# A graph attention pair on one core: scores of the second layer from h times (Wq'Wk) times h, keys made a chunk ahead

## The chip, the cores and the metric

One core of one Trainium2 chip runs the whole program. The metric is the device time of one execution in microseconds; the median of three runs is given. Engines: TensorE (PE), VectorE (DVE), ScalarE (ACT), GpSimd (POOL) and SyncE (SP), which issues most of the DMAs.

## The reference

Two layers over 8192 nodes with 128 features and one dense 0/1 matrix adj (8192 x 8192, int32):

```python
h = relu(layernorm(x))                       # layer 0: graph attention
wh = h @ W; e = leaky(wh @ a1 + (wh @ a2).T, 0.2); e = where(adj > 0, e, -9e15)
x = x + elu(softmax(e) @ wh)
h = relu(layernorm(x))                       # layer 1: cosine attention
Qn, Kn = cos_normalize(h @ Wq.T), cos_normalize(h @ Wk.T)   # x / max(norm, 1e-4)
att = softmax(where(adj > 0, Kn @ Qn.T, -9e15))
x = x + 0.5 * (mask * (att @ h) + (1 - mask) * h) + 0.5 * h # mask: the row has a neighbour
```

## The kernel before

The matrix adj is read twice, once for each layer, 1 MB at a time into slots of a ring.

**Layer 0** goes over eight chunks of 1024 rows; a chunk has 32 units of 2 x 128 neighbours. For each unit SP loads adj into one of 8 slots (L265), ScalarE turns it into 0/1 (Sign, L406), VectorE makes the weights with two operations (L808), and TensorE runs 48 matmuls (L1020) on f16 words split in a high and a low part. Each engine runs its own instruction queue in program order and waits on semaphores. VectorE and ScalarE do the epilogue of chunk c in pieces between the masks of chunk c+1 (quotient, elu, residual, LayerNorm, h split in two f16 parts in u_buf), at the units given in `parts`; x1 and h are written to DRAM.

**The transition.** Layer 1 needs, for all 8192 nodes, the normalised q and k, transposed, in q_buf and k_buf, each as two f16 parts. The nodes go in 16 blocks of 512. For a block SP loads h from DRAM (load_h, L286), TensorE transposes it (t2, L951, in f32), ScalarE copies the result (copy_ht, L496), TensorE multiplies with Wq' and Wk' side by side in f32 (qk, L1047), ScalarE squares the product (square, L510), VectorE sums the squares (norms, L822), ScalarE takes roots (root, L520), VectorE forms reciprocals and scales the product (scaled, L833), TensorE transposes q and k (t3, L1058), ScalarE copies the high parts (high, L515 and L516) and VectorE subtracts for the low parts (low, L840). GpSimd takes no part in this. The epilogue of the last chunk of layer 0 lies between blocks 0 to 7. One buffer holds the squares. The first two transpositions of h (t2) stand before the last group of eight units of layer 0. Layer 1 begins when block 15 is done.

**Layer 1** goes over 16 chunks of 512 rows, each with 16 steps of 4 x 128 neighbours: TensorE makes scores of a step in four banks (L1086, 12 matmuls of 512 columns in two halves), ScalarE exponentiates each half with one instruction over 1024 columns (exps, L554), VectorE masks with adj (L866), ScalarE rounds to f16 (high_part, L560), VectorE subtracts (low_part, L871), and TensorE multiplies with the h parts in u_buf (values, L1102 and L1107). The values run LAG = 3 steps behind the scores, so in the very first chunk scores of four steps come before the first values. Scores of a half wait for the exponentials of the same half one step earlier (s_e). The epilogue of a chunk is laid between the steps of the next (`parts` in chunk1).

Semaphores that matter below: s_used (unit consumed, frees a slot), s_ht and s_htc (h transposed, copied), s_sq (squares ready), s_lo (low parts ready), s_s, s_e, s_m, s_ph, s_pl (stages of a layer 1 step), s_hw (h written).

## Time and profile before

| | us |
|---|---|
| median of 3 runs (lowest to highest) | 2204.03 (2203.57 to 2205.78) |
| the profiled execution | 2204.63 |
| its span, first to last instruction | 2202.8 |
| TensorE matmuls busy | 2155.7 (98%) |
| VectorE busy | 1983.9 (90%) |
| ScalarE busy | 1641.0 (74%) |
| mean granted TensorE clock | 0.995 of 2.4 GHz |
| moved by DMA | 573.23 MB |

The sum of the busy times is no bound by itself: layer 0, the transition and layer 1 have different limits, and each stretch has to be looked at alone. Times in the rows are microseconds from the start of the span unless they are means in ns; L followed by a number is a line of the kernel.

### The profile page before, as it was taken

What the parts mean: (1) busy time and instruction counts of PE and PEld (TensorE: products, weight loads), DVE (VectorE), ACT (ScalarE), POOL (GpSimd) and SP (SyncE); (2) the same over time, 40 slices, a digit from 0 to 9 for tenths busy, and PEclk for the clock granted to TensorE, in tenths of its full rate; (3) what the DMA queues carried; (4) which work ended last, traced back from release to release, by engine and by line L of the source; (5) the groups of instructions that cost most, each with busy time, mean ns of one, the idle gap of its engine ahead of it and who ended that gap; (6) DMA issues with size and microseconds to landing.
All of it is one profiled execution on the core that took longest, in us unless ns stands there. A gap on an engine that the chain in (4) does not pass through costs nothing.

```text
span 2202.8 us, 62846 instructions
## 1 busy us (share of the span) xinstructions
PE 2155.7 (98%) x26133; PEld 1749.5 (79%) x26133; DVE 1983.9 (90%) x1701; ACT 1641.0 (74%) x1446; POOL 9.5 (0%) x25
## 2 busy tenths in 40 slices
PE   5999999999999979999999999999999999999998
PEld 5999999999999966777777777777777777777776
DVE  7999999999999799888888898898898888888887
ACT  6687778878787667777777777777777777777776
POOL 1000000000000000000000000000000000000000
PEclk9999999999999999999999999999999999999999
DMA  6899999999999824565665665656666656655653
GB/s 244 331 380 400 397 401 400 399 404 400 401 400 391 343 72 157 199 211 205 206 219 196 211 219 192 222 207 201 215 199 217 206 201 215 211 205 206 221 195 115
DMA packets 153483, 573.23 MB, mean 260 GB/s; under 512 B 9889, under 2 KB 10337, under 8 KB 152929
## 3 DMA queue, kind: packets, MB, share of 16 engines
q1 hardware_dynamic: 144096, 549.78, 68.6%
q10 hardware_dynamic: 9216, 20.98, 2.4%
q8 instruction: 132, 2.16, 0.4%
q14 instruction: 39, 0.31, 0.0%
HBM read 558.11 MB, written 12.62 MB: 259 GB/s over the span
## 4 chain that ended last, share of the span: by engine, by line
PE 94%; DVE 3%; ACT 1%; issue 1%; DMA 0%; SPq 0%; DVEq 0%; POOL 0%; ACTq 0%; POOLq 0%
PE bank L1020 32%; PE bank L1086 30%; PE bank L1107 21%; PE bank L1102 10%; DVE hl_buf L833 1%; PE bank L1047 0%; DVE hl_buf L645 0%; DVE hl_buf L657 0%; DVE norm L822 0%; DVE v_buf L840 0%; DVE q_buf L840 0%; DMA wqk_sb<-wqk 0%; ACT ring L554 0%; PE bank L951 0%; PE bank L1058 0%
## 5 line engine op out<-in xcount | busy, mean ns | idle before, releaser
L554 ACT ACTIVATE ring<-bank 128x1024 f32<-128x1024 f32 x512 | 523.7, 1023 | 348.8 <-PE bank L1086 346.5
L866 DVE SCALAR_TENSOR_TENSOR ring<-ring 128x2048 f32<-128x2048 int32 x256 | 586.4, 2291 | 158.7 <-ACT ring L554 158.7
L1020 PE MATMUL bank<-v_buf,ring 128*128 128x129 f16 (+1 forms) x12288 | 710.9, 220 | 6.3 <-DVE ring L808 6.1
L1020 PEld LDWEIGHTS bank<-v_buf,ring 128*128 128x128 f16 x12288 | 707.4, 98 | 9.8 <-issue 9.0
L1086 PE MATMUL bank<-v_buf,q_buf 128*128 128x512 f16 x3072 | 704.8, 379 | 2.3 <-ACT ring L554 1.3
L1107 PE MATMUL bank<-u_buf,hl_buf 128*128 (+1 forms) x8192 | 704.3, 220 | 0.0
L1107 PEld LDWEIGHTS bank<-u_buf,hl_buf 128*128 128x128 f16 x8192 | 631.9, 98 | 55.8
L808 DVE SCALAR_TENSOR_TENSOR ring<-r_ring,th_word,ring 128x1024 f32<-128x1024 f32 x512 | 619.8, 1276 | 22.7 <-ACT ring L406 22.3
L871 DVE TENSOR_TENSOR hl_buf<-ring,hl_buf 128x2048 f16<-128x2048 f32 x256 | 584.5, 2284 | 0.0
L1102 PE MATMUL bank<-u_buf,hl_buf 128*128 (+1 forms) x2048 | 557.9, 272 | 0.2 <-DVE hl_buf L871 0.2
L406 ACT ACTIVATE ring<-ring 128x2048 f32<-128x2048 int32 x256 | 481.2, 1908 | 94.5 <-DMA ring<-adj 90.9
L1086 PEld LDWEIGHTS bank<-v_buf,q_buf 128*128 (+1 forms) x3072 | 289.8, 98 | 305.4 <-issue 2.5
L560 ACT ACTIVATE hl_buf<-ring 128x2048 f16<-128x2048 f32 x256 | 487.0, 1902 | 0.6 <-DVE ring L866 0.6
L1102 PEld LDWEIGHTS bank<-u_buf,hl_buf 128*128 128x128 f16 x2048 | 197.0, 96 | 30.3 <-DVE hl_buf L871 0.4
L1047 PE MATMUL bank<-wqk_sb,hl_buf 128*128 128x256 f32 x128 | 34.2, 414 | 10.0 <-DVE hl_buf L833 9.6
L1047 PEld LDWEIGHTS bank<-wqk_sb,hl_buf 128*128 128x128 f32 x128 | 24.6, 202 | 16.3 <-ACT hl_buf L496 7.6
L465 ACT ACTIVATE hl_buf<-q_buf,nbias,rstd 128x128 f32<-128x128 f32 x64 | 25.9, 483 | 10.8 <-DVE nbias L636 10.8
L421 ACT ACTIVATE v_buf<-hl_buf 128x516 f16<-128x516 f32 x16 | 10.1, 639 | 25.0 <-DVE hl_buf L733 25.0
L951 PE MATMUL bank<-ident,hl_buf 128*128 128x128 f32 x128 | 21.5, 299 | 6.5 <-POOL hl_buf L357 4.1
L439 ACT ACTIVATE hl_buf<-bank,den 128x128 f32<-128x128 f32 x64 | 17.3, 381 | 10.5 <-DVE den L750 10.5
L951 PEld LDWEIGHTS bank<-ident,hl_buf 128*128 128x128 f32 x128 | 16.8, 154 | 9.5 <-POOL ident L348 4.1
L1058 PE MATMUL bank<-ident,hl_buf 128*128 128x128 f32 x128 | 18.5, 291 | 5.7 <-DVE v_buf L840 5.7
(106 smaller groups left out, 451.2 us busy)
## 6 DMA issues: line engine op xcount, KB each, us to landing
ring<-adj SPq DMA_DIRECT2D x512, 1024.0 KB, 5.7
r_ring<-a_rows SPq DMA_DIRECT2D x8, 512.0 KB, 7.1
x_dram<-q_buf ACTq DMA_DIRECT2D x8, 512.0 KB, 7.0
h_dram<-hl_buf ACTq DMA_DIRECT2D x8, 512.0 KB, 7.2
hl_buf<-h_dram SPq DMA_DIRECT2D x16, 256.0 KB, 2.7
r_ring<-x_dram ACTq DMA_DIRECT2D x16, 256.0 KB, 3.9
r_ring<-h_dram ACTq DMA_DIRECT2D x16, 256.0 KB, 4.1
out<-r_ring ACTq DMA_DIRECT2D x16, 256.0 KB, 4.4
```

The lines of the kernel that those rows point to most:

```text
L406: nc.scalar.activation(slot(k), slot(k, I32), ACT.Sign).then_inc(s_sg, 1)
L554: nc.scalar.activation(p_ring[:, k, hf * 1024:(hf + 1) * 1024], bank[:, 2 * hf:2 * hf + 2, :].rearrange("p b n -> p (b n)"), ACT.Exp, scal ...
L560: nc.scalar.activation(hl_buf[:, 0, k, :], p_ring[:, k, :], ACT.Copy).then_inc(s_ph, 1)
L808: ins = V.scalar_tensor_tensor(half, r_ring[:, par, :].rearrange("p (b n) -> p b n", b=2), th_word[:, 2 * u + jj:2 * u + jj + 1], half, AL ...
L866: V.scalar_tensor_tensor(p_ring[:, k, :], adj_ring[:, k, :], 0.0, p_ring[:, k, :], ALU.is_gt, ALU.mult).then_inc(s_m, 1)
L871: V.tensor_tensor(hl_buf[:, 1, k, :], p_ring[:, k, :], hl_buf[:, 0, k, :], ALU.subtract).then_inc(s_pl, 1)
L951: ins = nc.tensor.transpose(dst[:, f], src[:, f], ident[:, :])
L1020: ins = mm(acc0(par, it), weights0(k, ps)[:, it // 4, jj, f], v2[:, bass.ds((2 * j + us) * VW, D + 1)], start=False, stop=False, skip_grou ...
L1047: ins = mm(qk_banks(r)[:, k * 2 * D:(k + 1) * 2 * D], ht_ring[:, r, k * P:(k + 1) * P], wqk_sb[:, :], start=True, stop=True)
L1086: ins = mm(bank[:, 2 * hf + m, :], q_buf[:, qs, bass.ds(j * P, P)], k_buf[:, ks, bass.ds(i * IW, IW)], start=(x == 0), stop=(x == 2))
L1102: mm(acc1_wide(par, it), hl_buf[:, 0, k, f], v, start=head and m == 0, stop=False, skip_group_check=True)
L1107: ins = mm(o, hl_buf[:, ps, k, f], v.rearrange("p o c -> p (o c)"), start=False, stop=tail and m == 3 and (ps, us) == (1, 0), skip_group_c ...
```

## The change

- The scores use M = Wk'Wq (host input `wkq` holds Wk and Wq; one f32 matmul in chunk 1 of layer 0 makes the product). Scores are (M h_i) times h_j, so q_buf holds the plain transposed h in two f16 parts, and k_buf holds keys M h, multiplied for each row i by 1/norm of its k. The 1/norm of q_j is given to the exponential as a scale for each partition, so an exponential is now over one bank (512 columns), four per step.
- Both Wq/Wk and M are scaled by their largest size and split in f16 parts (sizes on ScalarE after unit 24 of chunk 1, an all-reduce on GpSimd, split_weights on VectorE after unit 27). h is lifted by 64 (LIFT_H) through the root of the LayerNorm.
- A block's transposition reads the f16 parts in u_buf directly (eight f16 transpositions, no load of h from DRAM); the copy takes both parts at once, even blocks on ScalarE, odd ones on VectorE. The product for the norms is 12 f16 matmuls of 256 columns. The scaling, the second transposition and the high and low parts of q are gone.
- Blocks 0 to 3 (EARLY) are multiplied inside the last chunk of layer 0: two transpositions before unit 22, and before each of units 27 to 30 one product and one transposition. The last chunk's loops over groups are written out.
- The squares have two buffers, both where h_ring and ht_ring lay; norm_sums (VectorE) gives 8 sums a block as before; roots and factors are taken for 16, 32 and 16 tiles at a time (FOLDS).
- Key factors have to lie along the columns: they are transposed on TensorE, written to DRAM (k_rows) and read back on all partitions into e_t (load_factors on ScalarE's queue; the first row by SP, which no longer loads h).
- Keys of chunk i+1 are made at the head of chunk i of layer 1: three matmuls of 512 columns (keys) into a bank of the value sums that are not yet begun; VectorE scales (key_scaled, after step 1), ScalarE rounds (key_high, at step 2), VectorE subtracts (key_low, after step 2). TensorE waits for s_ks before the first values of the chunk, and for s_lo before its first scores. Keys 0 are made in the transition and keys 1 in chunk 0.

```diff
+            def sizes():
+                act.wait_ge(s_w, 64)
+                nc.scalar.activation(w_tmp[:, 0:2 * D], wqk_sb[:, :], ACT.Abs, accum_out=w_scale[:, 0:1]).then_inc(s_wsum, 1)
+                act.wait_ge(s_m0, 1)
+                nc.scalar.activation(m_sb[:, :], bank[:, 7, 0:D], ACT.Copy).then_inc(s_wk, 1)
+                nc.scalar.activation(w_tmp[:, 2 * D:3 * D], bank[:, 7, 0:D], ACT.Abs, accum_out=w_scale[:, 1:2]).then_inc(s_wsum, 1)
...
+            def square(g):
+                act.wait_ge(s_qk, g + 1)
+                if g >= 2:
+                    act.wait_ge(s_red, g - 1)
+                nc.scalar.activation(sq_ring[:, g % 2, :], qk_banks(g), ACT.Square).then_inc(s_sq, 1)
...
+            quotient, exponential, ln_root, normalised = epilogue(NC0 - 1, 1)
+            copy_ht(0)
+            square(0)
+            copy_ht(2)
+            for g in range(1, EARLY):
+                square(g)
+            roots(0)
+            copy_ht(4)
             nc.scalar.activation(warm[:, :], ident[:, 0:1], ACT.Exp)
...
             quotient()
...
+            square(4)
             exponential()
...
+            nc.scalar.activation(warm[:, :], ident[:, 0:1], ACT.Sqrt)
+            copy_ht(6)
+            square(5)
+            copy_ht(8)
+            square(6)
+            square(7)
             ln_root()
...
+            copy_ht(10)
+            square(8)
+            normalised(0, IT0 // 2)
+            square(9)
+            normalised(IT0 // 2, IT0)
+            key_high(0)
+            square(10)
+            square(11)
+            roots(1)
             act.wait_ge(s_x1w, 16 * NC0)
...
+            copy_ht(12)
+            copy_ht(14)
+            for g in range(12, NI):
+                square(g)
+            roots(2)
+            nc.scalar.activation(warm[:, :], ident[:, 0:1], ACT.Exp)
+            act.wait_ge(s_hw, 16 * NC0)
...
-                    nc.scalar.activation(p_ring[:, k, hf * 1024:(hf + 1) * 1024],
-                                         bank[:, 2 * hf:2 * hf + 2, :].rearrange("p b n -> p (b n)"), ACT.Exp,
-                                         scale=1.0 / (UNIT * UNIT)).then_inc(s_e, 1)
+                    for m in range(2):
+                        j = 4 * (n % (T // 4)) + 2 * hf + m
+                        ins = nc.scalar.activation(p_ring[:, k, (2 * hf + m) * IW:(2 * hf + m + 1) * IW],
+                                                   bank[:, 2 * hf + m, :], ACT.Exp, scale=q_scale[:, j:j + 1])
+                    ins.then_inc(s_e, 1)
...
+                    parts = {(0, 2): lambda: key_high(i + 1), (1, 1): quotient, (2, 1): store, (2, 2): lambda: residual(i),
+                             (2, 3): lambda: load_factors(i + 2)}
...
+            def split_weights():
+                dve.wait_ge(s_wtop, 1)
+                tops, scales = w_scale[:, 2:4], w_scale[:, 4:6]
+                V.tensor_scalar(tops, tops, TINY, 1.0 / W_TOP, ALU.max, ALU.mult).then_inc(s_wk, 1)
...
+                dve.wait_ge(s_wk, 3)
+                for src, tmp, col in ((wqk_sb, 0, 4), (m_sb, 2 * D, 5)):
+                    n = src.shape[1]
+                    V.tensor_scalar(w_tmp16[:, 2 * tmp:2 * tmp + n], src[:, :], w_scale[:, col:col + 1], None,
...
+                dve.wait_ge(s_wk, 5)
+                for src, tmp, col in ((wqk_sb, 0, 4), (m_sb, 2 * D, 5)):
+                    n = src.shape[1]
+                    V.scalar_tensor_tensor(w_tmp16[:, 2 * tmp + n:2 * tmp + 2 * n], src[:, :], w_scale[:, col:col + 1],
...
+            def norm_sums(g):
+                dve.wait_ge(s_sq, g + 1)
+                V.reduce_sum(norms[:, :, 4 * g:4 * g + 4].rearrange("p s t -> p t s"),
+                             sq_ring[:, g % 2, :].rearrange("p (t s f) -> p t s f", t=4, s=2), AX.X).then_inc(s_red, 1)
...
+            def key_scaled(i):
+                dve.wait_ge(s_kt, i + 1)
+                dve.wait_ge(s_rk, 16 * (i + 1))
+                V.tensor_tensor(e_t, key_bank(i), e_t, ALU.mult).then_inc(s_ks, 1)
+            def key_low(i):
+                dve.wait_ge(s_hi, i + 1)
+                V.tensor_tensor(k_buf[:, 1, i * IW:(i + 1) * IW], e_t, k_buf[:, 0, i * IW:(i + 1) * IW],
+                                ALU.subtract).then_inc(s_lo, 1)
...
+            copy_ht(1)
+            norm_sums(0)
+            norm_sums(1)
+            copy_ht(3)
+            norm_sums(2)
+            norm_sums(3)
+            copy_ht(5)
+            factors(0)
             denominators()
+            copy_rows(0)
             negative()
...
+            copy_ht(7)
             residual()
...
+            norm_sums(4)
+            norm_sums(5)
             moments()
...
+            copy_ht(9)
+            norm_sums(6)
             scales()
...
+            norm_sums(7)
+            copy_ht(11)
+            key_scaled(0)
+            norm_sums(8)
             split()
...
+            key_low(0)
+            for g in range(9, 12):
+                norm_sums(g)
+            factors(1)
+            dve.wait_ge(s_x1w, 16 * NC0)
+            copy_ht(13)
+            copy_ht(15)
+            for g in range(12, NI):
+                norm_sums(g)
+            factors(2)
...
+                    parts = {(0, 1): lambda: key_scaled(i + 1), (0, 2): lambda: key_low(i + 1), (0, 3): some, (1, 1): kept,
+                             (1, 3): total}
...
+                if g >= 2:
+                    pe.wait_ge(s_hc[g % 2], g // 2)
+                for part in range(2):
+                    for k in range(4):
+                        ins = nc.tensor.transpose(ht_bank(g)[:, part * IW + k * P:part * IW + (k + 1) * P],
+                                                  u_buf[:, 4 * g + k, part * (D + 2):part * (D + 2) + D], ident16[:, :])
+                ins.then_inc(s_ht, 1)
+            def qk(g):
+                pe.wait_ge(s_hc[g % 2], g // 2 + 1)
+                if g == 0:
+                    pe.wait_ge(s_wk, 12)
+                    pe.wait_ge(s_free, NC0 - 1)
+                elif g <= EARLY:
+                    pe.wait_ge(s_sq, g)
+                elif g == EARLY + 1:
+                    pe.wait_ge(s_rr, 1)
+                    pe.wait_ge(s_free, NC0)
+                else:
+                    pe.wait_ge(s_sq, g - 1)
+                for k in range(4):
+                    for x, (hs, ws) in enumerate(parts):
+                        ins = mm(qk_banks(g)[:, k * 2 * D:(k + 1) * 2 * D],
+                                 q_buf[:, hs, g * IW + k * P:g * IW + (k + 1) * P], wqk16[:, ws, :],
+                                 start=(x == 0), stop=(x == 2))
+                ins.then_inc(s_qk, 1)
...
+            def keys(i):
+                if i >= 3:
+                    pe.wait_ge(s_fv, len(EPI1) * (i - 3) + EPI1.index("lows") + 1)
+                elif i == 2:
+                    pe.wait_ge(s_ks, 2)
+                for x, (hs, ms) in enumerate(parts):
+                    ins = mm(key_bank(i), m16[:, ms, :], q_buf[:, hs, i * IW:(i + 1) * IW], start=(x == 0), stop=(x == 2))
+                ins.then_inc(s_kt, 1)
...
+                early = {22: ((t2, 0), (t2, 1)), 27: ((qk, 0), (t2, 2)), 28: ((qk, 1), (t2, 3)),
+                         29: ((qk, 2), (t2, 4)), 30: ((qk, 3), (t2, 5))} if last else {}
...
+            qk(4)
+            t2(6)
+            transpose_factors(0)
+            for g in range(5, NI - 2):
+                qk(g)
+                t2(g + 2)
+                if g == 8:
+                    keys(0)
+            qk(NI - 2)
+            qk(NI - 1)
...
+                if 1 <= i <= NI - 2:
+                    keys(i + 1)
+                pe.wait_ge(s_lo, i + 1)
...
+                        if 1 <= i <= NI - 2:
+                            pe.wait_ge(s_ks, i + 2)
                         values(i, k - LAG, k - LAG, par, head=(k == LAG))
...
+                if first:
+                    keys(1)
+                    transpose_factors(2)
```

## Rows read from the trace of the kernel before

**Rows 1.** Busy us and instructions (x) of each engine in two stretches; PEclk is 1 at 2.4 GHz.
```profile
232.00:321.00 89.00, 89.00 (x1555) 89.00 (x1553) 86.11 (x91) 70.77 (x56) 0.00 (x0) 1.00 1.02 400
853.00:938.00 85.00, 85.00 (x839) 60.72 (x838) 75.03 (x34) 62.49 (x50) 0.00 (x0) 1.00 0.62 206
```

**Rows 2.** The chain that ended last, in order of time: start us, us, what.
```profile
203.79 540.00 PE bank L1020 x9408
```

**Rows 3.** Waits in the second layer, from 853 us on: us in total, times, longest.
```profile
ACT ring L554 <- PE bank L1086: 345.4, 489, 1.2
DVE ring L866 <- ACT ring L554: 157.3, 220, 0.8
```

**Rows 4.** Timeline of TensorE (start us, us, group) at the two ends of the transition.
```profile
744.51 22.18 PE L1020 MATMUL bank<-v_buf,ring 128*128 128x129 f16 x384
...
850.43 2.75 PE L1086 MATMUL bank<-v_buf,q_buf 128*128 128x512 f16 x12 [1.33 <-ACT ring L554]
853.02 0.27 PE L1102 MATMUL bank<-u_buf,hl_buf 128*128 128x258 f16 x1
853.13 0.39 PE L1107 MATMUL bank<-u_buf,hl_buf 128*128 128x129 f16 x4
```

**Rows 5.** Timeline of VectorE: two of the sums of squares in the loop of the transition.
```profile
817.62 1.21 DVE L822 TENSOR_REDUCE norm<-hl_buf 128x8 f32<-128x1024 f32 x1
...
821.51 1.21 DVE L822 TENSOR_REDUCE norm<-hl_buf 128x8 f32<-128x1024 f32 x1
```

**Rows 6.** Timeline of ScalarE: the second half of the first exponential.
```profile
842.63 1.02 ACT L554 ACTIVATE ring<-bank 128x1024 f32<-128x1024 f32 x1 [0.75 <-PE bank L1086]
```

**Rows 7.** Groups by form: busy us, mean ns of one, idle before and its releasers.
```profile
L554 ACT ACTIVATE ring<-bank 128x1024 f32<-128x1024 f32 x512 | 523.7, 1023 | 348.8 <-PE bank L1086 346.5
L560 ACT ACTIVATE hl_buf<-ring 128x2048 f16<-128x2048 f32 x256 | 487.0, 1902 | 0.6 <-DVE ring L866 0.6
...
L465 ACT ACTIVATE hl_buf<-q_buf,nbias,rstd 128x128 f32<-128x128 f32 x64 | 25.9, 483 | 10.8 <-DVE nbias L636 10.8
...
L822 DVE TENSOR_REDUCE norm<-hl_buf 128x8 f32<-128x1024 f32 x16 | 19.4, 1210 | 1.0 <-ACT hl_buf L510 1.0
...
L439 ACT ACTIVATE hl_buf<-bank,den 128x128 f32<-128x128 f32 x64 | 17.3, 381 | 10.5 <-DVE den L750 10.5
...
L768 DVE BATCH_NORM_STATS2 stats<-q_buf 128x6 f32<-128x128 f32 x64 | 13.1, 277 | 0.0
...
L455 ACT ACT_TABLE_LOAD x7 | 9.0, 1283 | 0.6 <-DVE q_buf L762 0.5
...
L755 DVE TENSOR_SCALAR hl_buf<-hl_buf 128x1024 f32<-128x1024 f32 x8 | 5.5, 686 | 2.2 <-ACT hl_buf L439 2.2
...
L840 DVE TENSOR_TENSOR q_buf<-bank,q_buf 128x512 f16<-128x512 f32 x8 | 5.5, 683 | 1.3 <-ACT q_buf L515 1.3
```

**Rows 8.** Timeline of VectorE: masks 20 to 24 of chunk 2 of layer 0.
```profile
288.50 12.04 DVE L808 SCALAR_TENSOR_TENSOR ring<-r_ring,th_word,ring 128x1024 f32<-128x1024 f32 x10
```

**Rows 9.** The DMA queue of SP (from its timeline) as the last chunk of layer 0 ends.
```profile
727.14 0.83 SPq L286 DMA_DIRECT2D hl_buf<-h_dram  x2
```

**Rows 10.** Timeline of ScalarE: masks 24, 25 and 31 of the last chunk of layer 0.
```profile
735.67 1.92 ACT L406 ACTIVATE ring<-ring 128x2048 f32<-128x2048 int32 x1 [3.71 <-DMA ring<-adj]
738.25 1.92 ACT L406 ACTIVATE ring<-ring 128x2048 f32<-128x2048 int32 x1 [0.66 <-DMA ring<-adj]
...
755.04 1.92 ACT L406 ACTIVATE ring<-ring 128x2048 f32<-128x2048 int32 x1 [0.66 <-DMA ring<-adj]
```

**Rows 11.** Timeline of VectorE: masks 20 to 29 of the last chunk of layer 0.
```profile
728.57 24.40 DVE L808 SCALAR_TENSOR_TENSOR ring<-r_ring,th_word,ring 128x1024 f32<-128x1024 f32 x20
```

**Rows 12.** DMA issues of the page: KB each, median us from issue to landing.
```profile
r_ring<-x_dram ACTq DMA_DIRECT2D x16, 256.0 KB, 3.9
```

**Rows 13.** Engines in short stretches of the transition, as Rows 1; PEclk before the last two columns.
```profile
770.00:775.00 5.00, 1.82 (x9) 1.30 (x9) 3.50 (x5) 3.99 (x6) 0.00 (x0) 1.00 0.18 52
775.00:780.00 5.00, 4.58 (x20) 3.81 (x19) 4.62 (x8) 2.09 (x4) 0.00 (x0) 0.66 0.09 20
785.00:790.00 5.00, 4.45 (x17) 3.40 (x15) 4.90 (x9) 1.37 (x4) 0.00 (x0) 0.56 0.00 0
```

More of the change, by code:

```diff
@@ L518, in root @@
-            def root(g):
-                act.wait_ge(s_n2, 3 * g + 1)
-                nc.scalar.activation(norm[:, 1, :], norm[:, 0, :], ACT.Sqrt).then_inc(s_nr, 1)
-            def block_of(g, r, head=False):
-                root(g)
-                square(g + 1, 1 - r)
-                copy_ht(g + 2, r)
-                if not head:
-                    high(g - 1)
-            square(0, 0)
-            exponential()
-            block_of(0, 0, head=True)
-            block_of(1, 1)
-            ln_root()
@@ L535, in _ @@
-            block_of(2, 0)
-            for g in range(3, 7):
-                block_of(g, g % 2)
-                normalised(2 * (g - 3), 2 * (g - 2))
-            block_of(7, 1)
-            act.wait_ge(s_x1w, 16 * NC0)
-            with act.Fori(0, NI // 2 - 5) as gg:
-                for r in range(2):
-                    block_of(2 * gg + r + 8, r)
-            root(NI - 2)
-            square(NI - 1, 1)
-            high(NI - 3)
-            root(NI - 1)
+            square(4)
+            exponential()
@@ L836, in low @@
-            def low(g):
-                for i, buf in enumerate((q_buf, k_buf)):
-                    dve.wait_ge(s_hi, 2 * g + i + 1)
-                    at = bass.ds(g * IW, IW)
-                    V.tensor_tensor(buf[:, 1, at], qkt_bank(i), buf[:, 0, at], ALU.subtract).then_inc(s_lo, 1)
-            def block_of(g, r, head=False):
-                norms(g)
-                if not head:
-                    low(g - 2)
-                scaled(g, r, start=head)
-            block_of(0, 0, head=True)
+            copy_ht(7)
@@ L893, in kept @@
                     dve.wait_ge(s_fin, 32 * (i + 1))
-                    if not (isinstance(i, int) and i == 0):
+                    if i == 0:
+                        dve.wait_ge(s_rw, 32)
+                    else:
                         dve.wait_ge(s_out, 16 * i)
@@ L926, in chunk1 @@
                         mask(n, k, turn)
-                        if first and g == k == 0:
-                            low(NI - 1)
-                        else:
+                        if not (first and g == k == 0):
                             low_part(n - 1, (k - 1) % RING)
-                        if isinstance(g, int) and (g, k) in parts:
+                        if (g, k) in parts:
                             parts[g, k]()
@@ L1009, in group @@
                         u = RING0 * g + k
+                        if last and u in early:
+                            for step, which in early[u]:
+                                step(which)
                         if peeled and k == 0 and not first:
@@ L1064, in _ @@
[L1064 to L1075 removed]
+                if c == 1:
+                    pe.wait_ge(s_wkq, 16)
+                    mm(bank[:, 7, 0:D], wkq_sb[:, 0:D], wkq_sb[:, D:2 * D], start=True, stop=True).then_inc(s_m0, 1)
@@ new lines, in chunk @@
+                if last:
+                    for g in range(1, G0):
+                        group(g)
+                else:
+                    with pe.Fori(0, G0 - 2) as h:
+                        group(h + 1)
+                    group(G0 - 1)
+            chunks0(chunk)
+            qk(4)
[7 more added lines that the diff above has]
+            qk(NI - 2)
@@ L1080, in scores @@
                 for hf in halves:
-                    if not start:
+                    if start:
+                        pe.wait_ge(s_sq, NI - 1 + hf)
+                    else:
                         pe.wait_ge(s_e, 2 * (n - 1) + hf + 1)
```

293 lines of the change are left out of this document (153 added, 140 removed).

## The prediction

> **What bounds the kernel now.** Read the stretches first: inside layer 0 (232 to 321) TensorE is busy 89.00 of 89 us, VectorE 86.1, ScalarE 70.8, the DMA engines full; inside layer 1 (853 to 938) TensorE is busy 85.00 of 85, VectorE 75.0, ScalarE 62.5 [rows 1]. Then the chain in order of time: one piece of 540.00 us with 9408 matmuls of layer 0 [rows 2], which is 57.4 ns a matmul and 2.755 us a unit (48 matmuls; 32 units a chunk). Then the waits of layer 1: ScalarE waits for TensorE's scores, VectorE for ScalarE's exponentials, 0.7 us each time [rows 3]; nobody keeps TensorE waiting. So both layers cost what TensorE costs, and only between them is there something else: layer 0 ends at 744.51 + 22.18 = 766.69, the first value matmul starts at 853.02 [rows 4]. Those 86.3 us are the transition. Its loop steps 821.51 - 817.62 = 3.89 us for each of 16 blocks, the sum of VectorE's six operations (two of 1.2, two of 0.7, two small) back to back [rows 5]. Its last part is a pipeline fill: the first exponential is complete at 842.63 + 1.02 = 843.65 [rows 6], 9.4 us before the first value matmul.
>
> The sum is made against the profiled execution: 2204.63 us, of which 2202.8 is span and 1.8 lies around it. The median of the three runs is 0.6 lower.
>
> **Unit costs.** Starts of consecutive operations lie about 0.1 us closer than their durations. ScalarE, 1024 columns from PSUM: 1.02, next one after 0.93; a conversion of 2048 1.90, spaced 1.8. Square and the even copies cost 0.95 in the walk. A pass of VectorE over 1024 columns (sum, two tensors) 1.21, spaced 1.13; over 512 from PSUM 0.68; table load 1.28 [rows 7]. TensorE: 12 matmuls of 512 columns take 853.02 - 850.43 = 2.59, 0.216 each; one of 258 columns holds it 0.11 (853.13 - 853.02) [rows 4]. So a new block product (12 of 256 columns, f16) is 1.32; a transposition of hi and lo is 8 of 128 columns at 57.4 ns, 0.46; keys of a chunk are 3 of 512 columns, 0.65.
>
> **Preparing the product Wk'Wq in layer 0.** One small matmul and three ScalarE operations in chunk 1 find room: ScalarE is idle a fifth of that stretch [rows 1]. VectorE gets 11 operations after unit 27: five tiny (0.17), three of 128 columns (0.35) and three of 256 (0.45, between 0.35 and the 0.68 of 512), 3.25 in all, 2.6 when they overlap as the others do. VectorE's lead over TensorE decides what of this shows. In chunk 2 TensorE starts unit 20 at 203.79 + 32 x 2.755 = 291.95 and VectorE has finished it at 288.50 + 2.4 = 290.9 [rows 2, 8]: 1.0 us of lead, the smallest of the chunk. So 1.6 us would come through if VectorE caught up nowhere, nothing if its few waits for ScalarE give way. I take **+1.2** (0 to 2.6). The all-reduce on GpSimd starts after ScalarE's unit 24 and is wanted after VectorE's unit 27, at least three of VectorE's units of 2.39 later; uncovered, its own length would be added, with VectorE's masks queued behind the wait. The squares' sums are VectorE's tensor_reduce before and after (GpSimd has no part in them in either), so that half of the change is free.
>
> **End of layer 0.** Two transpositions before unit 22, a block product and a transposition before each of units 27 to 30: 4 x 1.32 + 6 x 0.46 = 8.0 us of TensorE, moved ahead of the end; the two old transpositions (0.8) go. New waits stand in TensorE's queue there: product 0 wants ScalarE's copy, product 1 VectorE's, and both copies are queued behind these engines' last masks. In SP's queue the loads of h go; the queue issued them at 727.14 [rows 9], after waiting for a write of h, and the next mask waited 3.71 us for its data, so that mask 31 began at 755.04 [rows 10]. Without that mask 24 would begin some 3.1 us earlier (the next one waited 0.66), at 732.6, and seven more at 2.58 us bring ScalarE's last mask to 750.7, done at 752.6, and the first copy to 753.6; TensorE reaches product 0 at 743.8 (unit 24 before, 766.7 less 8 x 2.755 and the old transpositions) + 3 x 2.755 + 0.9 + 1.2 = 754.2, no wait. VectorE needs 2.39 a unit from 728.57 [rows 11]: done with unit 31 at 757.3, with the added 1.2 at 758.5, its copy at 759.8. TensorE comes to product 1 at 754.2 + 1.32 + 0.46 + 2.755 = 758.7 and waits **1.1** (0 to 5, if the masks still come late). Blocks 2 and 3 find their squares ready. New end: 766.7 - 0.8 + 8.0 + 1.2 + 1.1 = **776.2**.
>
> **The transition after it.** I walked the queues in program order from that end (T), with the unit costs. The epilogue of chunk 7 is unchanged: eight quotients 2.2, eight normalised tiles 3.2 (0.38 and 0.48 each, overlapped), moments 2.6 (eight statistics of 0.28 and six column operations), minimum 0.6, two residual passes 2.4, split 1.9 [rows 7]. Milestones: T+2.6 quotients done, product 5 starts 2.7; T+6.1 table switched back, copy 6; product 6 ends T+8.4; squares 5, 6, 7 end 8.0, 10.9, 11.9; root 13.1; square 8 waits for sum 6 at 15.0 (two squares buffers); normalised half and half 17.6 and 20.2 with square 9 between; split ends 22.2, low part of the keys 22.8; sums 9, 10, 11 end 23.9, 25.0, 26.2; roots 26.5, copy 12 at 27.5; products 12 and 13 end 28.9, 30.7; copy 15 at 32.4; product 15 at 34.1; sums 14 and 15 at 35.9 and 37.0; roots 37.3, table load and warm-up 38.8, residual loads issued 39.2. The first keys' row of factors takes a write and a read of 3.9 [rows 12], ready near T+9, wanted at T+17.7: hidden. By busy time alone VectorE has about 30.5 us in this (12 sums and five copies of 1.13, the epilogue, factors) and ScalarE 27; the walk's 39.2 is the dependencies between them, the low end is 30.
>
> A walk at full clock is short by what the clock takes. Before, TensorE was idle much of 770 to 775 (busy 1.8 of 5), then granted 0.66 and later 0.56, mostly the 1.2 GHz level [rows 13]. In the walk it is idle from T+20.5 to T+27.6 and from T+37.1 to T+40.4. I add **+4**: products 12 and 13 at half clock 2.6, a half of the first scores 1.3; 0 to 9 if all is slow until the first values.
> The Trainium skill says the same from the other end ("TensorE: Matmul & The Clock Gate", What's actually happening: the default is the throttled state and activity releases it); by that rule a thinner TensorE queue is the danger of this change, and 9 would be the term instead of 4.
> The Trainium skill ("VectorE: DVE Perf Modes", The perf-mode tier table) allows a copy from PSUM up to double rate, 16-bit data included. No row here has 16-bit data in PSUM; by the page a copy of 1024 would be near the 0.69 of the f32 pass in SBUF [rows 7], instead of 1.21, and the walk up to 2.5 shorter.
>
> Fill: exponentials are now four of 512 columns with a scale per partition. Two operands by pointer make 128 columns 0.48, one 0.38 [rows 7]; 1023 less 512 x 0.83 is 0.60, spaced 0.5, plus 0.1 for the pointer 0.6: **2.4 a step instead of 1.86**. From the start of the exponentials the fill is then: step 0 done 2.4, step 1 (scores follow half by half) 5.2, conversion 0 at 7.0, step 2 at 9.4, scores 3 at 10.8, and behind these stand the first values: **10.8**, with 2.4 + 9.4 as before = 11.8 as the high end.
>
> **Layer 1.** After the first values all is as before, 2202.8 - 853.0 = 1349.8, plus 15 chunks' keys on a full TensorE, 15 x 0.65 = **9.7**, and 0.3 of transposed factors. Hidden: ScalarE has 2.4 + 1.8 = 4.2 of the 5.29 a step; VectorE's scaling and low part of the next keys (0.6 each, one per step) fit its 0.7 of wait a step [rows 3], and TensorE wants the scaling only at step 3 of the chunk, some 9 us later. If that cover went, each late microsecond would show 15 times.
>
> **Sum.** T 776.2 + 39.2 + 4 = 819.4; + 10.8 = 830.2 (before 853.0, 22.8 earlier); + 1349.8 + 10.0 = 2190.0 span; + 1.8 = 2191.8; less 0.6, **2191**.
>
> **Rivals.**
> 1. Short chain: VectorE runs back to back after T and no clock is lost, 30 to 34 instead of 43: 2179 to 2186. For it, the old loop had VectorE without gaps [rows 5]; against it, three engines and two buffers of squares alternate. 0.2.
> 2. The transition hardly shrinks beyond what the keys cost: late masks (+4), half clock throughout (+5), or a copy chain longer than walked: 2197 to 2204. 0.13.
> 3. The other side: the split exponentials make ScalarE the bound of layer 1. Place: its step against TensorE's 5.29; from (5.29 - 1.8) / 4 = 0.87 us for each piece on. At 0.90 it costs 4 x 0.03 x 256 = 31 us: 2222. Against it, 0.6 from the nearest rows, though no row has 512 columns with a scale pointer. 0.06.
> 4. The shift does not do what it says: the scaled keys come late and TensorE waits at the head of each chunk, 1 us x 15: 2206. The 9 us of room speak against it. 0.03.
> My forecast, 2186 to 2197: 0.58.
>
> **Numbers.** The range 2180 to 2200 leaves out rivals 3 and 4, the far end of 2 and a bit of 1. Under 0.2% (4.4 us) a measurement of this kernel tells nothing: faster means under 2199.6, same up to 2208.4. Rival 3 is slower; rival 4 and the upper half of 2 are same: 0.85, 0.09, 0.06.
>
> **What would show it.** Layer 0's last matmul near 776; VectorE's last mask near 758; first exponential near 819 and first values near 830; PEclk under 1 in that stretch; exponentials at 0.6 to 0.7 each; key matmuls 0.65 a chunk, no new wait of TensorE in layer 1, so last matmul minus first values near 1354. Wrong if T lies past 781 (masks), if the first exponential comes more than 48 or less than 35 after T (walk), or if TensorE waits in layer 1.

## The result

| | before | after |
|---|---|---|
| median, us (4 runs each) | 2203.88 (2203.57 to 2205.78) | 2190.74 (2189.42 to 2192.20) |
| ratio | | 0.9939, 95% interval 0.9922 to 0.9956 |
| profiled execution: span | 2202.8 | 2189.5 |
| last matmul of layer 0 ends | 766.7 | 777.2 |
| first exponential | 839.9 | 817.3 |
| first values | 853.0 | 829.7 |
| first values to the end | 1349.8 | 1359.8 |

Forecast 2191, measured 2190.7. The clock times of the two traces can be set beside each other: layer 0 ends 10.5 us later, the first values (the first matmul that adds weighted rows of h in layer 1) come 23.3 us earlier, and what follows them is 10.0 us longer.

**Inside the layers.** The stretches of after that answer to [rows 1], first layer 1, then the whole transition from the last matmul of layer 0 to the first exponential (columns as there):

```profile
853.00:938.00 85.00, 85.00 (x835) 60.35 (x833) 75.21 (x44) 70.50 (x86) 0.00 (x0) 1.00 0.60 199
777.20:817.30 40.10, 27.60 (x241) 21.45 (x238) 28.40 (x52) 26.57 (x42) 0.00 (x0) 0.87 0.09 34
```

And the same transition of the kernel before:

```profile
766.70:839.90 73.20, 57.27 (x305) 46.39 (x305) 66.07 (x116) 49.34 (x95) 0.00 (x0) 0.93 0.18 58
```

In 853 to 938 TensorE is still busy all the time, ScalarE has gone from 62.5 to 70.5 us of 85. The transition fell from 73.2 to 40.1 us and VectorE's work in it from 66.1 to 28.4. That changes the character of the stretch: before, VectorE was busy 90% of it, now no engine is busy more than 71%. The waits of layer 1, for [rows 3] (who waits for whom: us in total, times, longest):

```profile
ACT ring L610 <- PE bank L1236: 220.9, 237, 1.6
DVE ring L979 <- ACT ring L610: 149.2, 221, 1.4
...
PE bank L1252 <- DVE hl_buf L984: 0.5, 1, 0.5
```

TensorE waits once in all of layer 1 after the first values, for 0.5 us.

**The end of layer 0 and the transition**, TensorE's timeline for [rows 4]: the two early transpositions, products 0 and 1, the last units, products 6 and 12, scores 1 to 3, the first values, and the keys of chunk 1.

```profile
739.53 1.06 PE L1125 MATMUL bank<-ident,u_buf 128*128 128x128 f16 x16
...
756.24 1.48 PE L1143 MATMUL bank<-wqk_sb,q_buf 128*128 128x256 f16 x12 [1.88 <-ACT q_buf L543]
...
760.76 1.47 PE L1143 MATMUL bank<-wqk_sb,q_buf 128*128 128x256 f16 x12
...
771.53 5.68 PE L1188 MATMUL bank<-v_buf,ring 128*128 128x129 f16 x96
...
784.10 2.74 PE L1143 MATMUL bank<-wqk_sb,q_buf 128*128 128x256 f16 x12 [2.28 <-ACT q_buf L543]
...
804.91 2.74 PE L1143 MATMUL bank<-wqk_sb,q_buf 128*128 128x256 f16 x12 [6.83 <-ACT q_buf L543]
...
818.65 6.96 PE L1236 MATMUL bank<-v_buf,q_buf 128*128 128x512 f16 x24 [2.79 <-ACT ring L610]
827.10 2.76 PE L1236 MATMUL bank<-v_buf,q_buf 128*128 128x512 f16 x12 [1.49 <-ACT ring L610]
829.70 0.27 PE L1252 MATMUL bank<-u_buf,hl_buf 128*128 128x258 f16 x1
...
832.40 0.81 PE L1163 MATMUL bank<-q_buf,m_sb 128*128 128x512 f16 x3
```

ScalarE's timeline there, for [rows 6, 10]: masks 29 and 31, copy 0, the second roots, the first exponential.

```profile
748.37 1.92 ACT L439 ACTIVATE ring<-ring 128x2048 f32<-128x2048 int32 x1 [2.10 <-DMA ring<-adj]
...
753.36 1.91 ACT L439 ACTIVATE ring<-ring 128x2048 f32<-128x2048 int32 x1 [0.63 <-DMA ring<-adj]
755.18 1.01 ACT L543 ACTIVATE q_buf<-bank 128x1024 f16<-128x1024 f16 x1
...
803.69 0.26 ACT L554 ACTIVATE ab_col<-ab_col 128x64 f32<-128x64 f32 x1 [1.29 <-DVE ab_col L909]
...
817.33 0.69 ACT L610 ACTIVATE ring<-bank,th_col 128x512 f32<-128x512 f32 x1
```

The chain shows the load behind mask 31 (start, us, what), then VectorE's timeline its last twelve masks and first copy, for [rows 11]:

```profile
746.14 7.14 DMA ring<-adj
```

```profile
729.56 28.78 DVE L893 SCALAR_TENSOR_TENSOR ring<-r_ring,th_word,ring 128x1024 f32<-128x1024 f32 x24
758.26 0.68 DVE L905 COPY q_buf<-bank 128x1024 f16<-128x1024 f16 x1
```

The forms that are new (mean ns of one after the busy time), for [rows 7]:

```profile
L610 ACT ACTIVATE ring<-bank,th_col 128x512 f32<-128x512 f32 x1024 | 648.1, 684 | 229.9 <-PE bank L1236 222.5
...
L1163 PE MATMUL bank<-q_buf,m_sb 128*128 128x512 f16 x48 | 13.0, 379 | 0.0
...
L905 DVE COPY q_buf<-bank 128x1024 f16<-128x1024 f16 x8 | 5.5, 685 | 6.9 <-PE bank L1125 6.9
```

### The profile page after: what moved, and what is told of

Its sections match the earlier page's. It is cut to its first block, busy times and chain, and to the rows that moved or that the text cites. A ratio compares the mean times of both kernels' runs of the same rounds, so it can differ in the third digit from the quotient of the medians.

```text
span 2189.5 us, 63171 instructions
## 1 busy us (share of the span) xinstructions
PE 2142.2 (98%) x26185; PEld 1734.1 (79%) x26185; DVE 1969.9 (90%) x1686; ACT 1753.8 (80%) x1928; POOL 10.6 (0%) x27
## 4 chain that ended last, share of the span: by engine, by line
PE 95%; DVE 3%; ACT 1%; DMA 1%; issue 0%; SPq 0%; ACTq 0%; POOL 0%; DVEq 0%
PE bank L1188 32%; PE bank L1236 30%; PE bank L1257 21%; PE bank L1252 10%; PE bank L1143 0%; PE bank L1163 0%; DVE hl_buf L705 0%; DVE hl_buf L717 0%; DVE ab_col L909 0%; DMA ring<-adj 0%; ACT ring L610 0%; DMA wqk_sb<-wqk 0%; PE bank L1125 0%; PE bank L1085 0%; ACT hl_buf L506 0%
## 5 line engine op out<-in xcount | busy, mean ns | idle before, releaser
L610 ACT ACTIVATE ring<-bank,th_col 128x512 f32<-128x512 f32 x1024 | 648.1, 684 | 229.9 <-PE bank L1236 222.5
L1143 PE MATMUL bank<-wqk_sb,q_buf 128*128 128x256 f16 x192 | 25.9, 290 | 12.9 <-ACT q_buf L543 11.0
L1143 PEld LDWEIGHTS bank<-wqk_sb,q_buf 128*128 128x128 f16 x192 | 19.0, 103 | 17.3 <-ACT q_buf L543 11.5
L909 DVE TENSOR_REDUCE ab_col<-hl_buf 128x8 f32<-128x1024 f32 x16 | 19.2, 1214 | 9.3 <-ACT hl_buf L549 9.2
L549 ACT ACTIVATE hl_buf<-bank 128x1024 f32<-128x1024 f32 x16 | 16.2, 1025 | 14.0 <-PE bank L1143 11.3
L626 ACT ACTIVATE r_ring<-bank,den 128x128 f32<-128x128 f32 x64 | 18.3, 376 | 6.6 <-DVE den L1001 6.6
```

What stands on the lines that cost most here:

```text
L610: ins = nc.scalar.activation(p_ring[:, k, (2 * hf + m) * IW:(2 * hf + m + 1) * IW], bank[:, 2 * hf + m, :], ACT.Exp, scale=q_scale[:, j:j ...
L1143: ins = mm(qk_banks(g)[:, k * 2 * D:(k + 1) * 2 * D], q_buf[:, hs, g * IW + k * P:g * IW + (k + 1) * P], wqk16[:, ws, :], start=(x == 0), ...
```

## The experiments

Eleven kernels; the table has their medians and, from their traces, the end of layer 0 (T), the first exponential (E) less T, first values (V) less E, and what follows V. In all of them the part after V is the same to 0.3 us unless the experiment touches it, so the profile places each change of time. The kernel before was run again beside each of the three groups of experiments (1 to 4, 5 to 8, 9 to 11) and had medians of 2204.0, 2204.2 and 2204.3; the kernel after was not.

| kernel | median us | T | E - T | V - E | after V |
|---|---|---|---|---|---|
| before | 2204.0 | 766.7 | 73.2 | 13.2 | 1349.8 |
| after | 2190.7 | 777.2 | 40.1 | 12.4 | 1359.8 |
| 1 sums twice | 2203.7 | 777.3 | 51.2 | 13.5 | 1359.8 |
| 2 squares twice | 2197.1 | 775.1 | 46.1 | 12.4 | 1359.8 |
| 3 keys twice | 2200.0 | 776.7 | 39.1 | 12.4 | 1369.6 |
| 4 before, exponentials split | 2204.8 | 767.0 | 71.5 | 13.9 | 1350.1 |
| 5 no early blocks | 2193.3 | 767.4 | 50.6 | 12.4 | 1359.8 |
| 6 copies first | 2183.7 | 774.9 | 35.1 | 11.0 | 1359.8 |
| 7 keep busy | 2187.2 | 776.2 | 38.8 | 11.0 | 1359.8 |
| 8 first copy | 2189.0 | 775.8 | 39.1 | 12.4 | 1359.9 |
| 9 both orders (6 and 8) | 2184.7 | 774.0 | 35.1 | 11.0 | 1359.8 |
| 10 lighter VectorE | 2185.8 | 775.2 | 35.9 | 13.5 | 1359.8 |
| 11 busy ramp | 2183.9 | 774.4 | 36.8 | 11.0 | 1359.8 |

T itself varies between kernels whose queues up to unit 22 are the same in order: the first early transposition begins between 738.1 and 739.7. So T is compared only together with that start. E - T varies too: it is 40.1 in after and 39.1 in experiments 3 and 8, which take nothing out of that stretch. The 1.0 us is the clock at product 6 (below, under The clock), and differences of that size in E - T are read with it in mind.

**1. Sums twice.**

```diff
+                V.reduce_sum(extra[:, :, 4 * g:4 * g + 4].rearrange("p s t -> p t s"),
+                             sq_ring[:, g % 2, :].rearrange("p (t s f) -> p t s f", t=4, s=2), AX.X)
                 V.reduce_sum(norms[:, :, 4 * g:4 * g + 4].rearrange("p s t -> p t s"),
```

> The changed kernel with every sum of squares in the transition done twice by VectorE (the extra result goes to an unused place): 12 more passes of 1.13 us after the end of layer 0, 13.6 us. My theory, that the new transition is a chain that alternates between ScalarE, VectorE and TensorE and passes through VectorE for about a third of it, expects the first values (829.7 now) 6 to 11 us later. If VectorE's own load were the bound, 13.6 later; if TensorE or ScalarE bounded it, less than 2.

The first exponential came 11.1 us later after T, the first values 12.4 in all, against 13.6 of added work. So the expected 6 to 11 for the first values was missed, and this run alone does not tell the chain from VectorE as the bound. (1.2 of the 12.4 lies in the ramp, the first steps of scores before any values: behind a wait of 5.06 us the next 24 score matmuls took 8.22 us, 6.96 in after.) Experiment 2 decides.

**2. Squares twice.**

```diff
+                nc.scalar.activation(sq_more[:, g % 2, :], qk_banks(g), ACT.Square)
                 nc.scalar.activation(sq_ring[:, g % 2, :], qk_banks(g), ACT.Square).then_inc(s_sq, 1)
```

> The changed kernel with every square in the transition done twice by ScalarE (extra result to an unused place): 12 more passes of 0.93 us after the end of layer 0, 11.2 us. The chain theory expects the first values 4 to 9 us later, since ScalarE's passes stand in the chain but share it with idle time; ScalarE as the bound expects 11, VectorE as the bound less than 2.

E - T is 6.0 us longer for 11.2 added (7.0 against the 39.1 of experiments 3 and 8, whose product 6 ran at full clock as it did here; 1.3 of that is product 13 at half clock, 2.73 us). The first values came 3.9 us later by the clock of the traces, since T was 2.1 earlier here, and the median is 6.4 higher. VectorE as the only bound, less than 2, is out. The two transitions, sums twice first, then squares twice (columns as above):

```profile
777.30:828.50 51.20, 28.65 (x240) 21.69 (x238) 41.44 (x64) 27.02 (x43) 0.00 (x0) 0.87 0.08 27
```

```profile
775.10:821.20 46.10, 28.16 (x240) 21.32 (x238) 28.62 (x52) 37.41 (x55) 0.00 (x0) 0.89 0.08 30
```

VectorE takes 41.4 of 51.2 us when loaded, ScalarE 37.4 of 46.1. Neither is a bound that hides the other: an added microsecond of VectorE costs 0.8, one of ScalarE 0.5 to 0.6. That is a chain that goes through both, more through VectorE.

**3. Keys twice.**

```diff
-                for x, (hs, ms) in enumerate(parts):
-                    ins = mm(key_bank(i), ...)
+                for again in range(2):
+                    for x, (hs, ms) in enumerate(parts):
+                        ins = mm(key_bank(i), ...)
```

> The changed kernel with the three key matmuls of every chunk done twice. If the keys lie fully on TensorE's path in layer 1, the stretch from first values to the end grows by 15 x 0.65 = 9.7 us, and the time by 9.7 to 10.4. The rival, that they fill time in which TensorE would wait anyway, expects less than 2.

1369.6 - 1359.8 = 9.8 us after the first values; the median is 9.2 higher, half a microsecond below the expected range. TensorE's key matmuls are on the path in full. That the other engines' part of the keys is hidden follows from what after itself shows: 10.0 us more behind the first values, no more than the matmuls.

**4. The kernel before with split exponentials.**

```diff
-                    nc.scalar.activation(p_ring[:, k, hf * 1024:(hf + 1) * 1024], ..., ACT.Exp,
-                                         scale=1.0 / (UNIT * UNIT)).then_inc(s_e, 1)
+                    for m in range(2):
+                        ins = nc.scalar.activation(p_ring[:, k, (2 * hf + m) * IW:(2 * hf + m + 1) * IW],
+                                                   bank[:, 2 * hf + m, :], ACT.Exp, scale=th_col[:, 0:1])
+                    ins.then_inc(s_e, 1)
```

> The kernel before, with each exponential of 1024 columns split in two of 512 that take their scale from a column (here the constant 1/4096). My theory: 0.5 to 1 us slower through the pipeline fill, nothing else, since ScalarE has room in every step. The rival (third in the prediction: ScalarE becomes the bound of layer 1) expects 5 us or more.

The scale (1/4096) is put into a column once, by a memset. Ratio to the kernel before 1.0004 (0.9994 to 1.0014); V - E 0.7 longer, the rest of layer 1 by 0.3. In 853 to 938 ScalarE is busy 70.6, TensorE still all of it:

```profile
853.00:938.00 85.00, 85.00 (x841) 60.71 (x839) 74.39 (x34) 70.60 (x84) 0.00 (x0) 1.00 0.62 203
```

**5. No early blocks.**

```diff
-                early = {22: ((t2, 0), (t2, 1)), 27: ((qk, 0), (t2, 2)), 28: ((qk, 1), (t2, 3)),
-                         29: ((qk, 2), (t2, 4)), 30: ((qk, 3), (t2, 5))} if last else {}
+                early = {24: ((t2, 0), (t2, 1))} if last else {}
...
+            for g in range(4):
+                qk(g)
+                t2(g + 2)
             qk(4)
```

(ScalarE's and VectorE's queues put the quotients, the exponential and the residual of the last epilogue between blocks 0 and 1.)

> The changed kernel without block work inside layer 0 but two transpositions: blocks 0 to 3 are multiplied, squared and summed after the end of layer 0, between the pieces of the last epilogue. Layer 0 should end 9 us earlier (8.0 - 0.9 of TensorE's work and its 1.9 us wait), near 768. Theory: block work costs about 2 us a block in the chain, so the first values come within 3 us of 829.7, and early blocks were worth little. The rival, that hiding blocks under layer 0 is the main part of the gain, expects 4 x 3.9 - 9, so 6 to 16 us later.

T 9.8 us earlier, the chain 10.5 longer: first values 0.7 later in the traces, the median 2.5 higher. The four blocks cost 2.6 us each in the chain (2.9 against the 39.1 of experiments 3 and 8). Hiding them under layer 0 is worth 0.7 to 2.5 us of the gain of 13, a fifth at most.

**6. Copies first.** ScalarE's queue (VectorE's alike: copy 13 after sum 9, copy 15 before the factors).

```diff
             square(10)
+            act.wait_ge(s_x1w, 16 * NC0)
+            copy_ht(12)
             square(11)
-            roots(1)
-            act.wait_ge(s_x1w, 16 * NC0)
-            copy_ht(12)
             copy_ht(14)
-            for g in range(12, NI):
+            square(12)
+            roots(1)
+            for g in range(13, NI):
```

> The changed kernel with the copies of blocks 12 and 13 put ahead of square 11 and of sums 10 and 11, and copies 14 and 15 ahead of the second roots and factors. In the trace TensorE idles 6.8 us before product 12, because copy 12 is queued behind roots that wait for three sums. Theory (queue order costs this): first values 3 to 5 us earlier, same in the time. Rival (VectorE's load after the split is the bound whatever the order): less than 1 us.

More than expected (the first values 8.7 earlier in the traces, 2.3 of it by T): E - T 5.0 shorter, and V - E another 1.4, which the expectation did not have. TensorE's waits before product 12 and before scores 1, then the clock of the ramp and the whole transition:

```profile
797.74 1.48 PE L1145 MATMUL bank<-wqk_sb,q_buf 128*128 128x256 f16 x12 [2.39 <-ACT q_buf L543]
...
811.31 5.59 PE L1238 MATMUL bank<-v_buf,q_buf 128*128 128x512 f16 x24 [2.69 <-ACT ring L611]
```

```profile
810.00:815.00 5.00, 3.62 (x16) 1.50 (x17) 2.29 (x1) 4.56 (x8) 0.00 (x0) 1.00 0.50 157
774.90:810.00 35.10, 26.33 (x240) 20.85 (x238) 28.12 (x52) 26.56 (x43) 0.00 (x0) 0.95 0.11 39
```

The 6.83 us before product 12 are 2.39, product 12 takes 1.48 us instead of 2.74, and the clock stays full in the ramp where after had 0.80 and 0.85. Median 2183.7, 7.1 below after. Not all of it is order: beside experiment 7, where the order is that of after and the clock full from product 12 on, E - T is 3.7 shorter and V - E the same.

**7. Keep busy.** keep_busy(n) is n matmuls of 512 columns whose result nobody reads.

```diff
+                if g == 11:
+                    keep_busy(24)
...
                     scores(i, 0, k, first and k == 0)
+                    if first and k == 0:
+                        keep_busy(12)
```

> The changed kernel with matmuls of no use (24 of 512 columns before product 12, 12 after the first scores) into a free bank, to keep TensorE's clock up. In the trace the clock is below full in 800 to 810 and 815 to 825, and product 12 and the second scores run at the half rate. Theory: first values 1.5 to 3 us earlier. Rival (the slow matmuls are hidden behind ScalarE and VectorE): no change, or up to 1 us later.

```profile
797.06 5.34 PE L1216 MATMUL bank<-q_buf,m_sb 128*128 128x512 f16 x24
804.05 1.48 PE L1143 MATMUL bank<-wqk_sb,q_buf 128*128 128x256 f16 x12 [1.65 <-ACT q_buf L543]
...
816.40 5.59 PE L1242 MATMUL bank<-v_buf,q_buf 128*128 128x512 f16 x24 [0.20 <-ACT ring L610]
```

With g = 11 they stand right before product 12. Product 12 takes 1.48 instead of 2.74, the two scores after the first 5.59 instead of 6.96. E - T 1.3 and V - E 1.4 shorter, median 3.6 lower: matmuls of no use, on the engine that bounds both layers, make the kernel faster, since they stand where it has nothing to do.

**8. First copy after mask 29.**

```diff
+                if c == NC0 - 1:
+                    parts[29] = first_copy
```

> The changed kernel with ScalarE's copy of block 0 put after mask 29 of the last chunk instead of after mask 31. TensorE waits 1.88 us for it, since mask 31 can only begin when slot 31, freed by unit 23, is filled. Theory: layer 0 ends 1.5 to 1.9 us earlier, and the first values with it. Rival (product 1 then waits for VectorE's copy, queued behind its last mask): the same 1.9 us turn up there and nothing is gained.

Product 0 no longer waits, product 1 waits 0.68 for VectorE:

```profile
753.99 1.47 PE L1147 MATMUL bank<-wqk_sb,q_buf 128*128 128x256 f16 x12
...
759.34 1.48 PE L1147 MATMUL bank<-wqk_sb,q_buf 128*128 128x256 f16 x12 [0.68 <-DVE q_buf L909]
```

From the first transposition to T it is 36.5 us instead of 37.7: 1.2 of the 1.9 are gained, 0.7 come back as the rival said. The median is 1.8 lower, but its runs (2187.2 to 2193.3) lie across all of those of after (2189.4 to 2192.2); the trace alone shows the gain.

**9. Both orders.** The edits of 6 and 8 together.

> The earlier copies of blocks 12 to 15 and the first copy after mask 29 together. If they save in different places (one after the end of layer 0, one before it), their gains add: chain from the end of layer 0 to the first exponential 35 as with the copies alone, wait before product 0 gone, time 1 to 2 us below the copies alone, near 2182.5. If VectorE's last mask takes back what the first copy gives, it stays at 2183.7.

In the trace they add (T less the first transposition 35.6, against 36.8 in 6; E - T 35.1, V - E 11.0; span 2179.9 against 2180.8). The 1 to 2 us expected in the time were not found: the medians, 2184.7 (2181.7 to 2187.2) and 2183.7 (2182.6 to 2185.6), don't tell the two apart.

**10. Lighter VectorE.** Experiment 9, with copy 15 moved to ScalarE and the factors of tiles 16 to 63 formed at once after the last sum.

```diff
-FOLDS = (0, 16, 48, T)
+FOLDS = (0, 16, T)
...
+            act.wait_ge(s_ht, NI)
+            nc.scalar.activation(both(15), ..., ACT.Copy).then_inc(s_hc[1], 1)
```

> As the one before, and VectorE relieved in the stretch where it has no gap: copy 15 goes to ScalarE (0.6 us), and the factors of tiles 16 to 63 are formed at once after the last sum and not in two parts (0.9 us less, 0.2 more at the end). If VectorE's load bounds the last 15 us, the first exponential comes 1.0 to 1.4 us earlier. If ScalarE's queue, now one copy longer, takes over, nothing or a loss.

The first exponential came no earlier: E - T 0.8 longer than in 9. The first theory is out as it stood. VectorE's last sums now wait for squares, which stand behind the added copy:

```profile
802.75 1.22 DVE L915 TENSOR_REDUCE ab_col<-hl_buf 128x8 f32<-128x1024 f32 x1 [1.68 <-ACT hl_buf L554]
804.77 2.35 DVE L915 TENSOR_REDUCE ab_col<-hl_buf 128x8 f32<-128x1024 f32 x2 [0.80 <-ACT hl_buf L554]
807.45 1.22 DVE L915 TENSOR_REDUCE ab_col<-hl_buf 128x8 f32<-128x1024 f32 x1 [0.33 <-ACT hl_buf L554]
```

But product 12 also took 2.47 us, behind the same wait of 2.39 after which it took 1.48 in 9, so how much of the 0.8 is ScalarE's longer queue and how much the clock stays open:

```profile
797.42 2.47 PE L1148 MATMUL bank<-wqk_sb,q_buf 128*128 128x256 f16 x12 [2.39 <-ACT q_buf L542]
```

TensorE then waited 3.41 us for the first exponentials, and its next scores, mostly at half clock, took 8.24 us where 6 has 5.59:

```profile
810.00:815.00 5.00, 2.65 (x7) 1.00 (x8) 1.85 (x3) 2.91 (x6) 0.00 (x0) 0.64 0.49 157
815.00:820.00 5.00, 5.00 (x18) 1.88 (x17) 1.79 (x2) 3.58 (x5) 0.00 (x0) 0.68 0.59 205
```

```profile
812.35 8.24 PE L1241 MATMUL bank<-v_buf,q_buf 128*128 128x512 f16 x24 [3.41 <-ACT ring L616]
```

**11. Busy ramp** (10 with `keep_busy(12)` behind the first scores).

> As the one before, with twelve matmuls of no use behind the first scores. In the run with earlier copies the clock was at full speed in all of the ramp, so they can gain nothing if the clock alone explains what they gave before: no change within 0.3 us, or up to 0.5 slower where they delay the second scores. If they help by something else, 1 us or more again.

V - E is 11.0 again, 2.5 less than in 10; so for this kernel the expectation was wrong, which took the clock of 6 for the clock of 10. E - T is 1.0 longer though nothing before E was changed: product 6 took 2.58 us here and 1.48 in 10. The median is 1.9 lower than that of 10, with overlapping runs (2182.1 to 2185.2 and 2182.5 to 2188.9), and no better than 6 or 9.

The best kernels are 6, 9 and 11, 6 to 7 us below after and some 20 below before; which of the three is best was not resolved.

## Why the prediction was right

Term by term: the end of layer 0 came 1.0 us later than put, the walk at full clock was about 1.4 shorter (an estimate, below), the clock took 3.7 instead of 4, the fill 0.2 more. Together that is 0.5 less, first values at 829.7 against 830.2. The mechanism held; that the time was met so closely is in part luck, since these errors cancel.

- **Both layers are TensorE's, the transition is not.** Held. Keys and transposed factors were put at 10.0 us behind the first values, measured 10.0; experiment 3 shows that they count in full.
- **Preparing the product.** VectorE's eleven operations were put at 2.6 us and took 223.02 - 220.72 = 2.3:

```profile
220.72 0.15 DVE L850 TENSOR_SCALAR w_scale<-w_scale 128x2 f32<-128x2 f32 x1
...
223.02 19.22 DVE L893 SCALAR_TENSOR_TENSOR ring<-r_ring,th_word,ring 128x1024 f32<-128x1024 f32 x16
```

  The first transposition begins 1.4 us later than unit 22 did before (743.63 - 2 x 2.755 = 738.1), which looks like the +1.2. But 0.5 of it was there when layer 0 began (its first unit starts at 55.29, before at 54.81). From the first unit to unit 22 it is 683.3 and 683.6 us in the two kernels without the product, 683.8 to 684.0 in eight kernels with it, and 684.2 (after), 684.7 and 685.1 in the other three. So the product itself shows as some 0.4 us, and the 1.2 was too high.
- **The end of layer 0.** 776.2 predicted, 777.2 found, but the wait stood in another place. I had TensorE wait 1.1 us for VectorE's copy at product 1 and not at product 0. It waited 1.88 for ScalarE's at product 0 and then no more. The failed term is "ScalarE's last mask done at 752.6": mask 31 began at 753.36 and was done at 755.3. I spaced the masks from the kernel before and did not ask when slot 31 would be free; but the two transpositions and the late start put the end of unit 23, which frees it, at 746, and its load took 7.14 us. What counts is slot freed + load + mask + copy, 746.1 + 7.1 + 1.9 + 1.0 = 756.2, against three units of TensorE. (Mask 29 had waited 2.10 for data besides.) Experiment 8 removes the wait by order. The other wait, 1.1 for VectorE's copy, did not come: TensorE was late by then, and the copy took 0.68, not 1.21.
- **The walk.** E - T was put at 39.2 with the clock's share apart, and 40.1 was measured with it inside. The milestones of after look as if they held one by one (starts, T 777.2): product 6 T+6.9, root for the last LayerNorm T+13.1 (13.1), second roots T+26.5 (26.5), product 12 T+27.7 (27.6), last roots T+38.3 (37.3). But product 6 ran at half clock in this trace, which the walk did not have. In experiment 8, where it ran at full clock, the same marks are T+6.9, T+12.6, T+25.5, T+26.7 and T+37.3, with product 12 still slow. So the walk at full clock is some 37.8 (estimate: 40.1 less 1.0 for product 6 and 1.3 for product 12), 1.4 shorter than mine. Experiments 1 and 2 show that it is a chain between the engines; that the old loop was VectorE's load is read from its queue (busy 90% of the old transition) and was not tested. The low end of 30 by busy time alone was no danger; it takes another order to get near it, and 35.1 is what order gave.
- **The copy from PSUM.** I used 1.21 us; the 16-bit copy takes 0.685, the length of the f32 pass in SBUF. The Trainium skill ("VectorE: DVE Perf Modes", The perf-mode tier table) allows it the double rate, and the trace agrees. How much of the 1.4 it explains no run shows. In experiment 8 ScalarE waits 0.84 us for VectorE before the root at T+12.6, with copy 7 in VectorE's stretch before it, so some of the first 0.5 may be the copy. Later TensorE waits for ScalarE's copy 12 before product 12, and VectorE's copy 15 waits 4.33 us for the transposition that TensorE has queued behind that product; a shorter copy on VectorE gives nothing there.
- **The clock.** Put at +4, seen at 3.7, in other places: products 12 and 13 were to be slow, 6 and 12 were. The low stretches of the kernel after (the third last column is PEclk), for [rows 13]:

```profile
785.00:790.00 5.00, 4.64 (x40) 3.80 (x39) 4.86 (x17) 2.38 (x3) 0.00 (x0) 0.77 0.05 21
...
805.00:810.00 5.00, 4.99 (x40) 3.89 (x40) 0.70 (x2) 1.73 (x2) 0.00 (x0) 0.72 0.00 0
815.00:820.00 5.00, 2.21 (x8) 0.72 (x7) 1.50 (x6) 4.14 (x7) 0.00 (x0) 0.80 0.38 131
820.00:825.00 5.00, 5.00 (x20) 1.81 (x19) 2.96 (x2) 3.45 (x5) 0.00 (x0) 0.85 0.42 127
```

  Product 12 (2.74 for 1.47) and scores 1 and 2 (6.96 for 5.59) ran wholly or partly at 1.2 GHz, after TensorE had been idle 6.83 and 2.79 us. Experiment 7 gives them back: 1.3 + 1.4. Product 6 took 2.74 as well, after 2.28 us of idle; in experiment 8 it took 1.48 after the same wait:

```profile
782.69 1.48 PE L1147 MATMUL bank<-wqk_sb,q_buf 128*128 128x256 f16 x12 [2.28 <-ACT q_buf L542]
...
802.49 2.74 PE L1147 MATMUL bank<-wqk_sb,q_buf 128*128 128x256 f16 x12 [6.82 <-ACT q_buf L542]
```

  E - T is 39.1 there and in experiment 3, which has product 6 at 1.48 too: the third part, 1.0. The Trainium skill ("TensorE: Matmul & The Clock Gate", What's actually happening) has the throttled clock as the default, released by activity, and the traces agree in direction. That an idle stretch alone decides they do not show: in 6 an idle time of 2.69 us before the same scores left the clock full, after a better filled stretch before it, and product 6 came out either way behind the same wait and the same work.
- **The fill and the exponentials.** 10.8 at full clock, measured 11.0 in the four kernels whose clock stayed up (6, 7, 9, 11). An exponential of 512 columns with a scale pointer takes 684 ns; four are spaced to 2.4 us, as put. Rival 3 is out: experiment 4, and ScalarE's 70.5 of 85 us in layer 1.
- **Rivals 1, 2 and 4** did not come: the chain was near the walked one, the keys were in time (TensorE waits once in layer 1 after the first values, 0.5 us). Rival 1's chain of 30 to 34 us gives 2178 to 2182 by the sum above it, not the 2179 to 2186 that stand there. With another queue order, 6, the chain is 35.1 and the clock nearly full; VectorE still had gaps (busy 28.12 of 35.10).

## What to carry to other kernels

When an engine's load is taken out of a serial stretch, what is left is a chain through several queues; walk it in program order with the durations of the trace, and look for an operation that someone waits for behind one that itself waits. Here a copy behind a batch of roots was worth more than the overlap with the layer before: 6 to 7 us, of which 3.7 is the wait itself and the rest the clock that the wait had cost, against 0.7 to 2.5. Cheap work moved onto the engine that bounds a long layer is paid in full however small it is: 0.65 us a chunk, 10 us in all, almost half of what the shorter transition gave.

## What was not expected of the hardware

- Idle TensorE time in a transition can cost twice, once as wait and once as slow matmuls behind it. V - E took three values in kernels with the same ramp of work but different work before it: 11.0, 12.4 and 13.5 us. Matmuls of no use in the gaps brought 12.4 and 13.5 back to 11.0 (experiments 7 and 11).
- The same wait can be followed by either clock. Product 6 came 2.28 us after TensorE's last work in after, 7, 3 and 8; it took 2.74 us in the first two and 1.48 in the last two, and the chain behind it was 1.0 us longer or shorter. A single trace of a serial stretch is no finer than that.
- f16 transpositions run at the pace of matmuls: 16 in 1.06 us, the last one's length included, in a stretch with a granted clock of 1.00 (735 to 745).
- Splitting the exponentials costs ScalarE's time but no time of the kernel, as long as each step has room: 512 pieces more and 8 us of 85 more work left layer 1 within 0.3 us of its old length (experiment 4).
